# Fused attention and expert kernel: ten dense products of a step regrouped into five adjacent pairs

## What is computed

```
h = token_mix(x)                      # causal decaying window of 32 tokens, then two dense layers
a = layernorm(h); q, k, v = a@wq+bq, a@wk+bk, a@wv+bv      # 16 heads of 16
scores = causal(q k^T / 4); weights = softmax(scores)
h = h + (weights v) @ wo + bo
h = h + ffn(layernorm(h))             # 2 shared experts and the top 2 of 16 routed ones
```

## Time and profile before

| what | value |
|---|---|
| median of 3 runs | 2182.4 us (2175.43 to 2186.65) |
| the profiled execution's own time | 2178.16 us |
| span of its trace | 2176.4 us |
| PE busy, whole span | 1868.5 us (86%) |
| DVE / ACT / POOL busy | 1382.1 (64%) / 973.0 (45%) / 958.8 (44%) us |
| mean granted TensorE clock | 0.93 of full speed |

### The profile page before, as it was taken

One profiled execution on the slowest core, in us unless ns is written; L12 is line 12 of the kernel. 1 busy time (PEld: TensorE's weight loads), 2 busy tenths in 40 slices (PEclk: granted clock), 3 DMA queues, 4 the chain that ended last, 5 costly groups with the idle time before them and its releaser, 6 DMA issues. The chain is left out here.

```text
span 2176.4 us, 48608 instructions
## 1 busy us (share of the span) xinstructions
PE 1868.5 (86%) x14417; PEld 1370.0 (63%) x14418; DVE 1382.1 (64%) x3805; ACT 973.0 (45%) x2062; POOL 958.8 (44%) x1315
## 2 busy tenths in 40 slices
PE   4799999999999999999999984888888868777774
PEld 4667777777777777777777643555555547666663
DVE  3577878778787877787787733655555542444444
ACT  1165656666565656656565641222222214333331
POOL 3044444444444444444444441444455540555555
PEclk7799999999999999999999975889899998989897
DMA  2333434333333433433343415222222216788886
GB/s 67 91 123 128 136 118 134 125 125 131 125 134 123 142 114 124 137 125 134 123 135 113 136 61 133 86 85 71 81 88 88 74 68 196 230 264 252 262 263 203
DMA packets 214514, 291.08 MB, mean 134 GB/s; under 512 B 44854, under 2 KB 176666, under 8 KB 214426
## 3 DMA queue, kind: packets, MB, share of 16 engines
q1 hardware_dynamic: 168634, 183.07, 27.1%
q0 software_dynamic: 18048, 49.31, 7.3%
q10 hardware_dynamic: 27744, 57.68, 7.1%
HBM read 83.25 MB, written 129.69 MB: 98 GB/s over the span
## 5 line engine op out<-in xcount | busy, mean ns | idle before, releaser
L809 DVE TENSOR_REDUCE neg_max<-bank 120x1 f32<-120x376 f32 (+2 forms) x896 | 521.1, 595 | 220.1 <-PE bank L585 218.4
L734 ACT ACTIVATE probs<-bank 128x376 f32<-128x376 f32 (+2 forms) x896 | 451.2, 522 | 282.8 <-PE bank L619 271.3
L585 PE MATMUL bank<-k_rows,q_rows 64*128 64x128 f32 (+2 forms) x1536 | 405.6, 339 | 14.4 <-ACT probs L734 9.5
L619 PE MATMUL bank<-q_rows,k_rows 64*120 64x120 f32 (+2 forms) x1536 | 391.7, 342 | 3.6 <-ACT probs L734 3.3
L928 POOL TENSOR_SCALAR_AFFINE_SELECT probs<-probs 128x512 f32<-128x512 f32 (+1 forms) x384 | 234.0, 629 | 275.1 <-ACT probs L734 275.1
L602 PE MATMUL bank<-causal,own_row 64*120 64x120 bf16 (+4 forms) x1792 | 289.3, 242 | 15.2 <-DMA k_rows<-k_flat_hi 11.4
L1731 POOL DMA_INDIRECT x_sorted<-r_normed,route x188 | 183.7, 977 | 210.0 <-DVE route L1582 158.2
L2081 POOL DMA_INDIRECT y_got<-y_sorted,p_route x188 | 182.5, 971 | 186.0 <-issue 177.4
L585 PEld LDWEIGHTS bank<-k_rows,q_rows 64*128 64x128 f32 (+1 forms) x1536 | 237.8, 187 | 27.4 <-ACT probs L734 21.1
L602 PEld LDWEIGHTS bank<-causal,own_row 64*128 64x128 bf16 (+2 forms) x1792 | 151.2, 114 | 137.1 <-issue 68.9
L619 PEld LDWEIGHTS bank<-q_rows,k_rows 64*128 64x128 f32 (+1 forms) x1536 | 229.2, 183 | 8.9 <-ACT probs L734 6.3
(11 more groups left out here) (204 smaller groups left out, 3804.8 us busy)
## 6 DMA issues: line engine op xcount, KB each, us to landing
x_sorted<-zeros ACTq DMA_DIRECT2D x32, 816.0 KB, 3.9
y_sorted<-zeros ACTq DMA_DIRECT2D x32, 816.0 KB, 4.9
x_rows<-x_sorted SPq DMA_DIRECT2D x51, 512.0 KB
y_sorted<-p_y_rows SPq DMA_DIRECT2D x51, 512.0 KB
q_rows<-q_flat_hi SPq DMA_DIRECT2D x256, 94.0 KB
k_rows<-k_flat_hi SPq DMA_DIRECT2D x256, 94.0 KB
q_rows<-q_flat_lo SPq DMA_DIRECT2D x128, 94.0 KB
k_rows<-k_flat_lo SPq DMA_DIRECT2D x128, 94.0 KB
```

The costliest lines, as they stand in the source:

```text
L585: last = eng.matmul(ps[0:T[t], m * w:(m + 1) * w], q[rows, slot, t * P:t * P + T[t]], k[rows, slot, 0:w], start=False, stop=(m == len(head ...
L619: last = eng.matmul(ps[0:T[t], m * w:(m + 1) * w], k[64 * c:64 * c + 64, slot, t * P:t * P + T[t]], q[64 * c:64 * c + 64, slot, t * P:S], ...
L734: eng.activation(probs[g % 2][0:T[t], first:first + len(heads), OFF[t]:OFF[t] + w], bank_exp[n % 2][0:T[t], 0:len(heads) * w].rearrange("k ...
L809: eng.tensor_reduce(dst, src, AX.X, ALU.max, negate=True).then_inc(max_taken, 1)
```

## The change

Each of five pairs of dense products now stands together behind one unit. hid0 moves from behind unit 1 to behind unit 2, next to hid1; maxT1 from 5 to 6, ahead of val0; nT0 from 8 to 9; q0 from 13 to 14; out1 stays at 23 and out0 moves there from 22. The readers on ScalarE and VectorE follow, and the last reciprocal of half 1 moves from n = 16 to n = 14.

```diff
@@ TensorE, step
-                        if n in (1, 2) and st.front:
-                            hid_rows(st, n - 1)
+                        if n == 2 and st.front:
+                            hid_rows(st, 0)
+                            hid_rows(st, 1)
...
-                        if n == 5 and st.attend:
+                        if n == 6 and st.attend:
                             max_T(st, 1, 0)
                         if n == 6 and st.maxima:
                             values(st, 0)
-                        if n in (8, 9) and st.front:
-                            normed_T(st, n - 8)
-                        if n in (13, 14) and st.front:
-                            query_key(st, "q", n - 13, w_q)
+                        if n == 9 and st.front:
+                            normed_T(st, 0)
+                            normed_T(st, 1)
+                        if n == 14 and st.front:
+                            query_key(st, "q", 0, w_q)
+                            query_key(st, "q", 1, w_q)
...
-                        if n in (22, 23) and st.finish:
-                            out_rows_(st, n - 22)
+                        if n == 23 and st.finish:
+                            out_rows_(st, 0)
+                            out_rows_(st, 1)
@@ ScalarE, step
-                        if n == 5 and st.attend:
-                            take_hi(st, "maxT1", maxT[0][0:8, 1, :], 8)
                         if n == 5 and st.finish:
                             keep(st, 3, -1)
+                        if n == 6 and st.attend:
+                            take_hi(st, "maxT1", maxT[0][0:8, 1, :], 8)
                         if n == 6 and st.front:
                             normalise(st)
-                        if st.front and n in (8, 9):
-                            take_hi(st, f"nT{n - 8}", nT[st.b % 2][0][:, n - 8, :])
-                        if st.front and n == 13:
+                        if st.front and n == 9:
+                            for j in range(2):
+                                take_hi(st, f"nT{j}", nT[st.b % 2][0][:, j, :])
+                        if st.front and n == 14:
...
-                        if st.front and n in (13, 14):
-                            j = n - 13
-                            take_hi(st, f"q{j}", q_flat[0][:, j, :], bias=bias_q[:, j:j + 1])
+                            for j in range(2):
+                                take_hi(st, f"q{j}", q_flat[0][:, j, :], bias=bias_q[:, j:j + 1])
@@ VectorE, step
-                HALF_1_AT, HALF_0_AT = (10, 11, 12, 13, 16), (22, 24, 25, 26, 27)
+                HALF_1_AT, HALF_0_AT = (10, 11, 12, 13, 14), (22, 24, 25, 26, 27)
...
-                        if n == 6 and st.attend:
+                        if n == 7 and st.attend:
                             take_lo(st, "maxT1", maxT[1][0:8, 1, :], maxT[0][0:8, 1, :], 8)
...
-                        if st.front and n in (14, 15):
-                            j = n - 14
+                        if st.front and n in (15, 16):
+                            j = n - 15
                             take_lo(st, f"q{j}", q_flat[1][:, j, :], q_flat[0][:, j, :], bias=bias_q[:, j:j + 1])
```

## The result

The changed kernel takes 2196.56 us (median of 22 runs, 2173.59 to 2220.89) against 2185.49 us before (22 runs, 2162.66 to 2211.23). The ratio, taken over the fast runs of each, is 1.0064, 95% interval 1.0042 to 1.0087: slower by some 14 us (the two medians lie 11.1 us apart). The forecast was 2187 against 2182.4, a ratio of 1.0021. The sign and the range (2169 to 2204) hold. The size is three times the forecast's 4.5 us: it is clear of no change at all, and the interval reaches over the 0.5% that the forecast took as its bound for "no change".

A forecast was written before the change was run, and what follows sets the result against it. PE looked like the bound (195.39 of 200 us busy), but handoffs between engines were taken to set the step. Savings of 0.28 a pair are repaid, leaving 0.15 us in each of 30 steps: 4.5 us, 2187 from 2182.4, range 2169 to 2204.

The forecast's parts named there:

- The pair's saving of 0.28: On PE, each pair put together saves about 0.28 us, 1.4 a step for five, if PE had nothing to wait for.
- The normalising is the gate, and unit 9's wait takes the gain back: At nT0: normalising 0.28 us earlier, but unit 9 waits for unit 7's exponential behind it; nT0 603.75, near 603.1 before.
- k0 waits for q0's rest: At k0: it needs q0's bank, read by VectorE until 612.67, so it starts 0.11 us later, at 612.72.
- 0.11 to 0.25: Bounds in us on how much longer each step becomes, through k0's shift and later signals to ScalarE.
- My 0.15: Value taken for the lengthening of each step, in us; over 30 steps 4.5 us slower.
- a held unit's signal: Units whose scores were held back should signal ScalarE later than ones that ran at once, by up to 0.1 us.
- the one sentence on maxT1's rows: SyncE's four row DMAs for half 1 start about 1 us later, needed by unit 14 some 4 us after; cost nothing.
- The faster rival: PE is the bound and part of the 0.28 a pair stays: -13 us, 2169, or 2140 if all stayed; chance 0.14.
- The Trainium skill's rule on draining: On PE: changing tiling mode drains TensorE, so every pair put together gains; by it alone 42 us less.
- The slower rival: At unit 23 and the out pair: ScalarE waits make PE late at conv0; 0.42 us a step, 2195; chance 0.22.
- That nothing is lost: At q0 and k0: q0 read in time, k0 unmoved; -0.05 to 0.05 us a step, 2182 within 2; chance 0.14.

The follow-up runs named there:

- 5: Changed kernel with only maxT1 put back behind unit 5, the other four pairs kept: 2045.59 us against 2036.02 for the kernel before, ratio 1.0025.
- 6: Kernel before with the hid pair alone put together: ratio 1.0007 to the kernel before, step 37.56 us against 37.84.
- 12: Kernel before with the out pair alone put together: ratio 1.0016 to the kernel before, step 37.84 us, unchanged.
- Experiment 1: Changed kernel with ScalarE's two page clearings moved from n = 9 and 11 to 12 and 14: 2182.57 us against 2178.21 for the kernel before, ratio 1.0054.
- 4: Changed kernel with the last reciprocal of half 1 back at n = 16: 2202.80 us, ratio 1.0116 to the kernel before.
- 10: Changed kernel with the old order in the steps up to b = 0: 2054.37 us, ratio 1.0083 to the kernel before.
- 8: Kernel before with the nT pair alone put together: ratio 0.9997 to the kernel before, step 38.01 us against 37.84.
- 3: Changed kernel with nT0 and nT1 back behind units 8 and 9: 2217.07 us, ratio 1.0182 to the kernel before.
- 11: Kernel before with the maxT1, val0 pair alone put together: ratio 1.0035 to the kernel before, step 38.02 us against 37.84.
- experiment 9: Kernel before with the hid pair alone, only from step 1 on: 2032.31 us against 2036.38 for the kernel before, ratio 0.9971.

## Why the prediction was right, and where it failed

It was right in sign and in most of its stations. But what it described makes 0.08 of the 0.49 us a step; the other 0.41 came from a term that it had put at nothing. That the time still fell inside the range is luck as far as that term goes: the range reached to 2204 for the out pair, not for the rows. Medians over some 25 steps, us after conv1:

| station | before | worked out | after | maxT1 undone (5) |
|---|---|---|---|---|
| nT0 starts | 14.11 | 14.74 | 14.71 | |
| rounded part of nT0 | 14.84 | 15.70 | 15.64 | |
| rest of nT0 | 15.86 | 16.24 | 16.16 | |
| maxima of unit 11 | 17.71 | 18.09 | 18.02 | |
| q0 starts | 18.61 | 19.50 | 19.89 | 19.48 |
| k0 starts | 23.59 | 23.71 | 24.08 | 23.67 |
| step | 37.84 | 37.95 | 38.33 | 37.92 |

*The pair's saving of 0.28* holds for hid, by 6; for the other four no run shows it as time.

*The normalising is the gate, and unit 9's wait takes the gain back.* It holds to 0.03 us at nT0. The normalising is 0.24 earlier (12.43 to 12.19) where 0.28 was worked out. ScalarE and VectorE show the handoffs of the prediction, in the changed kernel:

```profile
617.93 1.58 ACT L717 ACTIVATE normed<-hid,row_shift_by,rstd 128x256 f32<-128x256 f32 x3 [0.29 <-POOL row_shift_by L947]
619.42 1.01 ACT L739 ACTIVATE probs<-bank 120x480 f32<-120x480 f32 x2
621.41 0.86 ACT L708 ACTIVATE normedT_hi<-bank 128x376 fp32r<-128x376 f32 x2 [0.23 <-PE bank L535]
...
621.93 0.55 DVE L799 TENSOR_TENSOR normedT_lo<-bank,normedT_hi 128x376 fp32r<-128x376 f32 x1 [0.43 <-ACT normedT_hi L708]
```

The exponential of unit 7 starts 1.49 us behind the normalising (617.93 to 619.42), as in the earlier trace rows, and releases unit 9 at 620.02, after 0.91 us of waiting where 1.2 was foreseen.

*k0 waits for q0's rest*: it does, and by 5 the four pairs hid, nT, q and out together leave +0.08 a step, just under the lower bound of 0.11 to 0.25. My 0.15 was on the wrong side: of the up to 0.1 more for a held unit's signal nothing shows.

**The step that failed** is the one sentence on maxT1's rows: "SyncE's four row DMAs for half 1 start about 1 us later, but unit 14 needs them only some 4 us after that; I cost this at nothing". The delay of the issues was right: the first is 12.98 us into the step before (601.99) and 13.94 after (619.67), and the last rows' issue ends 2.1 us ahead of unit 14's masks. The margin was right too: by 1.2 us from issue to landing the last row would have come at 623.46, some 1.2 ahead of the scores at 624.63, and "about a microsecond more" is what would use that up. But nothing was put on the landing itself. The last two rows came behind the clearing of `x_sorted`, which is on another queue, and the last took 2.7. Its price is 38.33 - 37.92 = 0.41 us a step, 12 us in all, and with the 0.08 of the rest it is the 0.49. What a moved step passes has to include a queue that shares only the DMA engines with its own.

*The faster rival* (PE is the bound) is refuted: PE's busy time fell, and the step grew. The Trainium skill's rule on draining (TensorEngine Tiling, Key Properties) gives the right sign for hid, 0.28 a step. The drain itself no row shows, and as a rule for the kernel's time it fails wherever PE then waits: of the other pairs none brought anything. *The slower rival* reached near the right figure (2195) by the wrong mechanism: its place was the out pair, and 12 shows that the out pair costs 0.00; conv0 waits for the output rows as before and only carries k0's shift. *That nothing is lost* falls with the interval.

## What to carry to other kernels

When a dense step is moved, list its DMAs with their new issue times, and beside them every large transfer of the other queues: small rows, the last of which had landed in 1.2 us, took 2.7 once 816 KB on another queue had been issued ahead of it. Saving time on the busiest engine counts only ahead of the chain that sets the step: of five like pairs, one gained 0.28 us a step, one gained or lost nothing, and the others cost 0.17 to 0.18 each, so each is best tried alone and read from the median step. Two moves can hide each other's price when they share a bank, as maxT1 and nT0 do: undoing one of them made the changed kernel worse.

## What was not expected of the hardware

**Short drops of the granted clock.** In three steps of the changed kernel's profile the clock fell to the 1.2 GHz level for some 3 us, near 201.9, 389.7 and 1004.1 us (two are in the first table of rows: 0.72 and 0.66 as means of 6 and 5 us). Those steps took 41.98, 39.40 and 39.43 us and not 38.33. The kernel before has none between 117 and 1250 us. Experiment 1 had two (steps of 39.43 and 39.41), which explains in part why its time fell less than its steps. One of them, by windows of 1 us (columns as above):

```profile
306.00:307.00 1.00, 0.76 (x7) 0.63 (x8) 1.00 (x3) 0.85 (x3) 1.00 (x2) 1.00 0.00 0
307.00:308.00 1.00, 1.00 (x9) 0.68 (x8) 0.88 (x3) 0.93 (x3) 1.00 (x2) 0.56 0.04 11
308.00:309.00 1.00, 1.00 (x8) 0.72 (x7) 0.71 (x2) 0.65 (x2) 0.91 (x2) 0.50 0.03 8
...
311.00:312.00 1.00, 1.00 (x22) 0.59 (x14) 0.45 (x2) 0.19 (x1) 0.00 (x0) 1.00 0.00 0
```

and PE's timeline there, in the same kernel:

```profile
306.25 0.38 PE L585 MATMUL bank<-k_rows,q_rows 64*128 64x256 f32 x1 [0.94 <-ACT probs L739]
306.67 1.14 PE L535 MATMUL bank<-ident,normed 128*128 128x128 f32 x6
```

PE waited 0.94 us for the exponential of unit 7, the new wait of this change, and then the clock was at half; the nT pair took 1.14 us and not the 0.87 of the changed kernel's timeline above. Most steps have the same wait and no drop. The first drop of the changed kernel, at 201.9, came behind a wait of 2.34 us for a row of the maxima: in that step the last row's issue lasted until 197.03 and stood behind both clearings (`y_sorted`'s is issued at 195.81), and it landed at 200.73. Experiments 4 and 10, which leave this order as it is there, have the same wait in the same step (2.13 and 2.12 us) and a drop behind it each (201.4 and 195.6), in steps of 41.78 us; so this one repeats. Behind the wait of 0.94 us, 4 had one more drop and 10 none. Where the wait itself is the same as in other steps, a drop costs 1.1 us (1.5 in experiment 1; that unit 14 has no wait for the rows there, which could take some of it up, is a likely reason and not shown); in the step with the long wait, 3.65 us are lost, of which about 2.1 are the wait. That is some 6 us in the profiled execution. The Trainium skill (TensorE: Matmul & The Clock Gate, What's actually happening) says that the clock follows how busy the engine has lately been; the rows agree with that in direction. Experiments 5 and 8, whose longest wait on an exponential was 0.6 us between 240 and 1100 us, had no drop in these steps; but 3, with waits of 0.8 and 1.1 us on other things, and 11, with 0.8, had none either, so what decides it stays open.

**The filling.** conv1 of step 0 starts at 134.57 us before and 140.30 after, with the granted clock between 60 and 140 us at 0.85 and 0.77 (first rows). Seven kernels with the hid pair in step 0 stand at 139.7 to 144.5, which looks like its doing. But of seven with the old order there, five stand at 132.7 to 134.6 and two at 143.1 (experiment 9) and 145.3 (11), and experiment 10, at 134.3, was no faster for it. This stays open: one profile of each kernel does not tell whether the order or the single execution sets the clock there. So the account of the 14 us rests on the steps (14.7), while the profiled executions, 22.1 us apart, add 5.7 of filling and some 6 for the three drops, and give some back after the attention phase (conv1 of step 28 is 25.7 us later).
